# Conditional linear attention: keys kept token-major on 128-token tiles, one batch maximum, state summed in PSUM

## The reference, cut to what matters

```python
xn = _ln(x, ln_w, ln_b)                                   # over the 512 features
q = xn @ Wq + bq
k = xn @ Wk + bk + (1.0 - src_mask) * -1000000.0
q = softmax(q per head, over its 64 features)
k = softmax(k, over the 2048 tokens)                       # a maximum and a sum per feature
v = (xn @ Wv + bv) * src_mask
att = einsum('bnhd,bnhl->bhdl', k, v)                      # 64 x 64 per head
y = einsum('bnhd,bhdl->bnhl', q, att)
emb_out = silu(emb) @ W_emb + b_emb                        # emb: 2 x 1024, W_emb: 1024 x 1024
scale, shift = split(emb_out)
hh = _ln(y, ln2_w, ln2_b) * (1 + scale) + shift
return x + silu(hh) @ W_out + b_out
```

## Time and profile before

| | |
|---|---|
| median of three runs | 542.65 us |
| span of the profiled execution | 540.9 us |
| PE busy | 491.8 us (91%) |
| DVE busy | 400.0 us (74%) |
| ACT busy | 252.1 us (47%) |
| POOL busy | 137.1 us (25%) |
| mean granted TensorE clock | 0.975 of full speed |

### The profile page before, as it was taken

One profiled execution on the slowest core, in us unless ns is written; L12 is line 12 of the kernel. 1 busy time (PEld: TensorE's weight loads), 2 busy tenths in 40 slices (PEclk: granted clock), 3 DMA queues, 4 the chain that ended last, 5 costly groups with the idle time before them and its releaser, 6 DMA issues.

```text
span 540.9 us, 7156 instructions
## 1 busy us (share of the span) xinstructions
PE 491.8 (91%) x2458; PEld 399.2 (74%) x2458; DVE 400.0 (74%) x964; ACT 252.1 (47%) x455; POOL 137.1 (25%) x108
## 2 busy tenths in 40 slices
PE   2698999999999999869798999999999997778797
PEld 1487888888887557658686888888888886758585
DVE  6569979878396388868975796996965468996852
ACT  3665436437163126654660653544641332937450
POOL 0170030030030000845472400301203000284474
PEclk9799999999999999979899999999999999898999
DMA  8802002000320320024443120010000001004154
GB/s 267 278 2 98 1 20 78 0 19 2 109 106 0 105 90 2 1 93 141 156 144 128 59 79 20 6 73 20 0 1 0 1 17 62 0 2 157 39 197 153
DMA packets 19576, 36.87 MB, mean 68 GB/s; under 512 B 1708, under 2 KB 1752, under 8 KB 19544
## 3 DMA queue, kind: packets, MB, share of 16 engines
q1 hardware_dynamic: 17416, 32.27, 18.2%
q10 hardware_dynamic: 2128, 4.19, 2.4%
HBM read 28.07 MB, written 8.39 MB: 67 GB/s over the span
## 4 chain that ended last, share of the span: by engine, by line
PE 59%; DVE 23%; ACT 7%; DMA 6%; issue 5%; SPq 0%; ACTq 0%; DVEq 0%
PE ps L884 15%; PE ps L886 15%; PE ps L885 15%; PE ps L889 7%; DMA ekTm<-in_L_cond_Wq_dram 3%; PE ps L958 3%; PE ps L985 3%; DVE yst_b L529 2%; DVE yst_a L527 2%; DVE ekT L721 2%; DVE qs L600 2%; DMA x_in<-in_x_dram 1%; DVE yst_raw L498 1%; PE ps L1067 1%; DVE qmax L603 1%
## 5 line engine op out<-in xcount | busy, mean ns | idle before, releaser
L475 POOL TENSOR_TENSOR z_lo<-z,z_hi 128x512 fp32r<-128x512 f32 x32 | 42.3, 1358 | 210.8 <-ACT z_hi L250 210.8
L884 PE MATMUL ps<-zT_hi,wk_hi 128*128 128x512 f32 x128 | 51.8, 405 | 1.5 <-DVE res L727 1.5
L488 POOL TENSOR_TENSOR res<-res,bo_all 128x512 f32<-128x512 f32 x32 | 43.1, 1356 | 33.4 <-DMA res<-in_x_dram 33.4
L885 PE MATMUL ps<-zT_lo,wk_hi 128*128 128x512 f32 x128 | 51.0, 398 | 0.0
L884 PE MATMUL ps<-z_hi,ek_hi 128*128 128x512 f32 x128 | 50.0, 391 | 0.8 <-DVE ek_lo L611 0.8
L886 PE MATMUL ps<-zT_hi,wk_lo 128*128 128x512 f32 x128 | 50.8, 397 | 0.0
L884 PE MATMUL ps<-wq_hi,zT_hi 128*128 128x512 f32 x128 | 50.5, 395 | 0.0
L886 PE MATMUL ps<-wq_hi,zT_lo 128*128 128x512 f32 x128 | 50.2, 392 | 0.0
L885 PE MATMUL ps<-wq_lo,zT_hi 128*128 128x512 f32 x128 | 49.9, 390 | 0.0
L886 PE MATMUL ps<-z_hi,ek_lo 128*128 128x512 f32 x128 | 49.9, 390 | 0.0
L885 PE MATMUL ps<-z_lo,ek_hi 128*128 128x512 f32 x128 | 49.8, 389 | 0.0
(11 more groups left out here) (163 smaller groups left out, 1192.4 us busy)
## 6 DMA issues: line engine op xcount, KB each, us to landing
res<-in_x_dram SPq DMA_DIRECT2D x32, 256.0 KB, 3.0
out_dram<-res SPq DMA_DIRECT2D x32, 256.0 KB, 2.5
x_in<-in_x_dram SPq DMA_DIRECT2D x7, 1024.0 KB, 5.1
mrow<-in_mask_BxSx_fk_dram SPq DMA_DIRECT2D x8, 256.0 KB, 3.2
x_in<-in_x_dram ACTq DMA_DIRECT2D x2, 512.0 KB, 4.3
g_acc<-in_L_cond_Wk_dram ACTq DMA_DIRECT2D x1, 1024.0 KB, 8.9
ekTm<-in_L_cond_Wq_dram ACTq DMA_DIRECT2D x1, 1024.0 KB, 16.7
wv_sc<-in_L_cond_Wv_dram ACTq DMA_DIRECT2D x1, 1024.0 KB, 21.5
```

The costliest lines, as they stand in the source:

```text
L475: pool.tensor_tensor(z_lo[:, t, :], z[:, t, :], z_hi[:, t, :].bitcast(F32), ALU.subtract).then_inc(s["z_lo_ok"], 1)
L488: pool.tensor_tensor(res[:, t, :], res[:, t, :], bo_all[:], ALU.add).then_inc(s["res_b"], 1)
L884: pe.matmul(o, a[0], bb[0], start=start, stop=False)
L885: pe.matmul(o, a[0], bb[1], start=False, stop=False)
```

## The change

Nearly every function is rewritten. What it does:

- First pass, in 16 tiles of 128 tokens per batch instead of 4 chunks: per tile 4 transposes of z, 12 products for k and 12 for q (q of the last four tiles comes after all of k). Both have zT stationary and the weights moving, so k is **token-major** and `turn_k` is gone. All 16 tiles of k stay in SBUF (`kf`), an elementwise maximum over tiles is kept in `kmx`.
- After the last tile the maximum is transposed, reduced to one value per feature, and spread over all partitions by transposes (`turn_kmax`, `spread_kmax`). Nothing is rescaled any more.
- Then the G products of all 16 tiles run as one block, summing in four PSUM banks, with the masked z as stationary operand; so G needs neither `g_acc` nor its 16 transposes per batch.
- x is loaded a second time in this block, and normalised and masked again by DVE (`masked_z`), because z is normalised in place.
- The sum of exp(k) per feature is made on POOL over tiles (`add_den`), and the subtraction of q's head maximum moves from DVE to POOL (`q_shift`).
- The bias of v is folded into Wv (`wv_mod`); weight preparation moves between engines and into the first tiles of batch 0.
- The condition product is issued in four groups of 32 columns of the array, at tile 5 of batch 0, its weights loaded at the start.

The core of the diff (new lines; what they replace is printed above):

```diff
 # PE
+            def product_k(b, n):          # product_q alike, with wq and bank Q0 + n % 2
+                m = T * b + n
+                pe.wait_ge(s["zT_lo_ok"], m + 1)
+                if n >= 2:
+                    pe.wait_ge(s["k_sum"], m - 1)
+                for f in range(NB):
+                    last = split_product(ps[:, K0 + n % 2, :], (zT_hi[:, n % NT, f, :], zT_lo[:, n % NT, f, :]),
+                                         (wk_hi[:, f, :], wk_lo[:, f, :]), f == 0, f == NB - 1)
+                last.then_inc(s["k_ps"], 1)
+            def condition():
+                for h in range(2):
+                    pe.wait_ge(s[f"wemb_in{h}"], 16 * NTE)
+                    for t in range(NTE):
+                        last = pe.matmul(ps[32 * (t % 4):32 * (t % 4) + 32, M0 + h, :], semb[:, t, :], wemb[NTE * h + t],
+                                         start=(t < 4), stop=(t >= 4))
+            def product_g(b, n):
+                m = T * b + n
+                pe.wait_ge(s["zm_lo_ok"], m + 1)
+                pe.wait_ge(s["ek_lo_ok"], m + 1)
+                for j in range(NB):
+                    last = split_product(ps[:, A + j, :], (blk(zm_hi[:, n % NT, :], j), blk(zm_lo[:, n % NT, :], j)),
+                                         (ek_hi[:, n % NT, :], ek_lo[:, n % NT, :]), n == 0, n == T - 1)
+                last.then_inc(s["g_ps"], 1)
 ...
+                for n in range(T):
+                    if n + 1 < T and (b or n):
+                        turn_z(b, n + 1)
+                    product_k(b, n)
+                    if n < T - NT:
+                        product_q(b, n)
 ...
+                product_q(b, T - 4)
+                turn_kmax(b)
+                product_q(b, T - 3)
+                spread_kmax(b)
+                product_q(b, T - 2)
+                product_q(b, T - 1)
+                for n in range(T):
+                    product_g(b, n)
+                turn_q(i0, lambda j: None)
+                products_att(b)
 # DVE: one tile of the first pass, then the G block
+                for n in range(T):
+                    if n + 1 < T:
+                        zT_low(b, n + 1)
+                    c, t = n // NT, n % NT
+                    if c + 1 < NC:          # t 0, 1: two tile statistics each; 2: x_finish; 3: x_masked
 ...
+                    k_tile(b, n)            # PSUM + penalty + bias, then the running maximum
+                    if n < T - NT:
+                        q_add(b, n)
+                        q_top(b, n)
 ...
+                k_less_max(b, 0)
+                k_less_max(b, 1)
+                q_add(b, T - 2)
+                q_top(b, T - 2)
+                ek_low(b, 0)
+                q_add(b, T - 1)
+                q_top(b, T - 1)
+                masked_z(b, 4)
+                for n in range(T):
+                    if n + 2 < T:
+                        k_less_max(b, n + 2)      # kf - kmax_all, both in SBUF
+                    if n + 5 < T:
+                        masked_z(b, n + 5)        # tensor_scalar on x_in, in place
+                    if n + 1 < T:
+                        ek_low(b, n + 1)          # kf - ek_hi, both in SBUF
 # POOL
+                for n in range(T):
+                    if n + NT < T:
+                        zm_low(b, n + NT)         # x_in - zm_hi
+                    if n:
+                        add_den(b, n)             # den + kf[n]
 # ACT, G block: exp_k and ek_high of tile n + 2, then zm_high of tile n + 4, which waits for g_ps of tile n
+                for n in range(1, T):
+                    if n + 2 < T:
+                        exponentials_k(b, n + 2)
+                    if n + NT < T:
+                        zm_high(b, n + NT)
 # SP: chunk 1 of x of batch 1 goes where res lay
+                if b:
+                    for t in range(NT):
+                        sp.wait_ge(stored[t], 16 * i0)
+                    load_x(b, 1)
```

More of the change, by code:

```diff
@@ L144, in cond_linear_attention @@
[L144 to L160, removed]
+        res = x_in[:, 1]
@@ new lines, in cond_linear_attention @@
+        gT = x_in[:, 0]
+        eqT = [kf[:, 0:NT], kf[:, 3 * NT:4 * NT], kf[:, 0:NT], kf[:, 0:NT]]
+        y = [kf[:, NT:2 * NT], x_in[:, 0], kf[:, NT:2 * NT], kf[:, NT:2 * NT]]
+        hT = [(ek_hi[:], ek_lo[:]), (zm_hi[:], zm_lo[:])]
+        th = [kf[:, 2 * NT + f, :] for f in range(NB)]
+        u = [kf[:, 3 * NT + f, :] for f in range(NB)]
+        wk_raw, wq_raw, wo_raw = kf[:, 0:NT], eq[:, 0:NT], eq[:, NT:2 * NT]
+        wemb = [eq[:, T // 2 + t, :] for t in range(NTE)] + [kf[:, T // 2 + t, :] for t in range(NTE)]
@@ L305, in exp_q @@
-            def exp_q(i, c, t):
-                act.wait_ge(s["q_shift"], NT * i + t + 1)
-                to = eq[:, c * NT + t, :] if isinstance(c, int) else \
-                    eq[:, bass.ds(c * NT + t, 1), :].rearrange("p o d -> p (o d)")
-                act.activation(to, qs[:, t % 2, :], ACT.Exp).then_inc(s["q_exp"], 1)
-            def ek_high(i):
-                for t in range(NT):
-                    act.wait_ge(s["ek_ps"], NT * i + t + 1)
-                    copy(ek_hi[:, t, :], ps[:, A + t, :], "ek_hi_ok")
@@ new lines, in _ @@
+                for n in range(T - NT):
+                    q_shift(b, n)
+                    if b == 0 and n < NB:
+                        if n == 0:
+                            pool.wait_ge(s["lnb_wq_step"], 2 * NB - 1)
+                            pool.wait_ge(s["wv_in"], 16)
+                            pool.wait_ge(s["lnbw_ok"], 1)
+                        weighted(lnb_wv, wv_mod, lnb_w, "lnb_wv_step", n)
+                for n in (0, 1):
+                    zm_low(b, n)
+                q_shift(b, T - 4)
@@ new lines, in product_q @@
+            def product_q(b, n):
+                m = T * b + n
+                if n >= 2:
+                    pe.wait_ge(s["q_sum"], m - 1)
+                elif m == 0:
+                    pe.wait_ge(s["bk_ok"], 1)
+                elif b:
+                    pe.wait_ge(s["o_ok"], NT * (NC * b - 1) + n + 1)
+                for f in range(NB):
+                    if m == 0:
+                        pe.wait_ge(s["wq_lo_ok"], f + 1)
+                    last = split_product(ps[:, Q0 + n % 2, :], (zT_hi[:, n % NT, f, :], zT_lo[:, n % NT, f, :]),
@@ L931, in products_g, with spread_bias @@
[L931 to L941 removed]
+            def spread_bias(rows, step, bank):
+                pe.wait_ge(s[step], 2 * NB - 1)
+                pe.matmul(ps[:, bank, :], ones[:], rows, start=True, stop=True).then_inc(s["bias_ps"], 1)
@@ L979, in products_out @@
                     last.then_inc(s["o_ps"], 1)
-            def condition(h, bank, tiles=range(NTE)):
-                for t in tiles:
-                    n = NTE * h + t
-                    pe.wait_ge(wemb_in[n], 16)
-                    last = pe.matmul(ps[0:B, bank, :], semb[:, t, :], wemb[n % NW], start=(t == 0), stop=(t == NTE - 1))
-                if tiles[-1] == NTE - 1:
-                    last.then_inc(s["emb_ps"], 1)
             def ready(name, n):
```

989 lines of the change are left out of this document (426 added, 563 removed).

## The result

The changed kernel takes 566.87 us (median of 4 runs, 566.06 to 568.51). The kernel before took 543.08 on the same chip, and the ratio is 1.042 with a 95% interval of 1.038 to 1.046: slower, as forecast, and 7 us above the predicted 560. The sum was made on spans, from first to last instruction: it said 559.9, the profiled span is 565.2.

What follows compares the result with a forecast made beforehand. PE was taken to bound the first pass, with waits on DVE and ACT in the second passes. Terms -15.7 - 5.3 - 4 + 5 + 40 - 1 = +19 on 540.9 us gave 561.6 as median, forecast 560, range 524 to 574.

Steps and rivals of the forecast that it cites:

- Step 5: G block: DVE and POOL exclude each other, 4.25 us per tile against PE's 2.73; +19.9 per batch, +40 for both.
- Step 2: Condition product in four column groups: gain between 0 and 10.5 us; the middle, -5.3, was taken.
- Rival C: Condition product: column groups don't overlap, 565 us; if they do, 555; no own chance, within the forecast's 0.60.
- Steps 3 and 4: Earlier start of the first k product, -4 us; first-pass waits of PE on other engines, net +5, between 0 and +12.
- step 1: PE transposes: turn_k's 128 and G's 32 go, the maximum adds 8 per batch; -15.7 us.
- Step 4: First pass, both batches: PE stays the bound, with seams and waits on other engines; net +5 us, between 0 and +12.
- Step 6: g_acc, alpha, rescaling and mask product: 0; second pass, order unchanged, loses eight condition-row transposes and a DVE copy: -1 us.
- Rival A: G block: DVE and POOL overlap enough, so only its start costs; 526 us, faster; chance 0.19.
- Rival B: G block: PE's clock falls to half, a tile takes 5.46 us; 587 us; chance 0.07.
- The half-way case: G block: DVE and POOL overlap partly, 3.5 us per tile; 542 to 546 us, no change; chance 0.14 for 532 to 549.

Runs made afterwards that it cites:

- the run with 4 columns: Against the kernel after, POOL's add_den works on 4 of its 512 columns, leaving out most of the sum of exp(k); 548.09 us, ratio 1.006.

## Why the prediction was right, and where its sizes were off

The direction and the mechanism held: the change takes PE work away and lets POOL and DVE shut each other out where they feed the G products. That the total came within 7 us owes much to errors of opposite sign, and so does the direction. With the G blocks as measured (+22.8 for both, not +40) and every other term as forecast, the sum is +2 us, no change. It came out slower because other stages cost more than the forecast had them.

To compare by stages, the condition product has to be split. In the kernel before, its first half stands ahead of the first y product, from 175.81 to 182.77, 6.96 us. The second half stands between y products of the second pass, 3.52 + 3.53 = 7.05 us:

```profile
182.77 0.50 PE L884 MATMUL ps<-wq_hi,zT_hi 128*128 128x512 f32 x1
...
196.40 1.88 PE L985 MATMUL ps<-x_in,semb 128*2 128x512 f32 x4 [0.69 <-ACT z L250]
...
199.92 2.06 PE L958 MATMUL ps<-att,z 128*128 128x130 f32 x16
201.91 1.88 PE L985 MATMUL ps<-ekT,semb 128*2 128x512 f32 x4
...
205.44 2.06 PE L958 MATMUL ps<-att,z 128*128 128x130 f32 x16
```

The kernel after has all of it ahead of the first y product. With the forecast's middle (14 - 5.3 = 8.7 us there) the steps say, and the spans show:

| stage | predicted | measured |
|---|---|---|
| start of batch 0 to its first y product | +12.8 | 206.44 - 191.5 = +14.9 |
| batch 1, the same | +14.1 | 166.24 - 156.90 = +9.3 |
| both second passes | -8.1 | -2.6 + 2.6 = 0 |
| sum | +19 | +24.3 |

- *Step 5, the G block: too large.* Predicted 4.25 us per steady tile and +19.9 per batch; measured 3.75, and +10.9 and +11.9. The term that failed is the price of a POOL operation. I took its whole duration, 1.29 us; DVE loses 1.04 for it, because DVE's next operation starts before POOL's ends and is over 0.28 us after it. The 0.5 us per tile that this saves is 4 us per batch. The start of the block I had 6.6 us late; the blocks without add_den are 45.4 to 45.7 us, 1.7 to 2.0 above 43.7, so most of that was not there. The same sum says why it is enough to take out add_den, one of POOL's two operations: 1.67 + 1.04 = 2.71, just below PE's 2.73, and the run with 4 columns showed it.
- *Step 2, condition product: the other end.* Predicted -5.3 as the middle between 0 and -10.5; measured -10.3 (13.9 to 3.6 us). Rival C's other branch, 555, was the right one for this term. The rule that stood beside it (the Trainium skill, TensorEngine Tiling (Array Packing), Key Properties: different tiles load and multiply in parallel) agrees with this trace, 3.6 us against 13.9.
- *Steps 3 and 4, first pass of batch 0: far too small.* Take the G block (10.9), the condition product (3.6 in place of 6.96, -3.4) and the transposes (-7.85, half of step 1) out of the +14.9, and +15.2 remain where I had -1. I had priced DVE's work there against its slack (+3 for tiles 3 and 4), but not who comes before it: Wv's bias row stands behind POOL's seven weighting operations, which run between the q_shift operations, and PE stood 6.68 us for them; DVE's copies of the condition's rows stand behind q_top(6), another 2.90. After each wait PE's clock was lowered for a while: over the windows around the two, the granted clock is 0.72 and 0.74. A new order of the same work gave back 10.9 us of span to the first G product. The other 4 us can lie in the wait on POOL's weighting of Wq at 25.59 (3.3) and in the 16 products for the condition's columns (2.75 at 82.06), which stand in this pass now and had no term; no run tests either by itself.
- *Step 4, batch 1.* Take the G block (+11.9) and the transposes (-7.85) out of +9.3, and +5.3 remain, where I had about +2. The wait for x's chunk 1 was there: PE stood 2.9 us for the normalised x in this pass, as the sum had it (some 3 us). The tile behind it ran at a granted clock of 0.83 over 7.2 us, which the sum left out. The rest is open.
- *Step 6, second pass: wrong.* I said that the change leaves its order alone. In batch 1 it doesn't: the kernel before has the q turns between the second and the third y tile, the kernel after behind all four, and the pass became 2.6 us longer. In batch 0 the order is the same, but the half of the condition product that stood between the y tiles is gone, and PE now waits 3.88 us for DVE at this place. By its -7.05 and step 6's -1 the pass should be 8.1 us shorter; it is 2.6 shorter. The run with the turns moved in both batches took 5.1 us off the total, and 2.2 and 1.9 us off the two passes. About half of the 8 us stays open.
- *Step 1* was not tested by itself, so its -15.7 is argued. PE's busy time fell by only 5.3 us, but it also counts what ran at a lower granted clock.
- *Rival A* (overlap) is out: DVE was never idle in the steady tile. *Rival B* is out too: the granted clock was 1.00 in the G block of batch 0 and 0.97 in that of batch 1, with PE idle for about 1 us in each tile. The half-way case at 3.5 us per tile was nearer to the measured 3.75 than my 4.25 in the block itself. Its total of 542 to 546 missed only because the other stages cost more.

## What to carry to other kernels

Before work goes to a second engine, ask whether the two can run side by side at all: here two POOL operations per tile cost DVE 2.08 us of 3.75, more than the transposes had saved, and taking one of them out brought back 19 of the 24 us. A sum over the rows of a product that exists already can ride along as one or two columns in place of an engine's pass over the data. Work that is taken off a stage bound by waits gives back less than its length: here 8 us of it gave back 2.6. When preparations are rearranged, list for each wait of the bounding engine everything queued ahead of the producer: here steps moved by one tile were worth 12 us.

## What the runs showed of the hardware

- A shut-out DVE operation hides its wait in its duration (1.52 to 1.78 us in place of 0.54 to 0.68), with no idle time shown.
- A POOL tensor_tensor on 512 columns with two full inputs takes about 1.3 us, and two of them per tile kept DVE from its work for 1.04 us each on average; a third, with POOL's queue full, added 0.82. On 4 columns it took 0.20 us with DVE idle and 0.65 where it had to wait for k_less_max: the exclusion works both ways.
- POOL's memset took 0.53 us for 512 columns and 1.38 for 1536, and shut out a tensor_scalar but not a tensor_tensor.
- POOL's q_shift, whose second input is 8 values spread over 64 columns each, took 1.04 us, not the 1.3 of the operations with two full inputs.
- Small products with 2 moving columns cost 0.22 us each, and behind 3.5 us of them PE's granted clock was 0.53 in batch 0 and 0.81 in batch 1, although PE had not been idle.
- Four column groups of TensorE ran at 3.9 times the speed of one.
